# Means of lone rows as one TensorE product per group, and one VectorE division per four tiles, in layers 1 to 3 of a graph-attention kernel

## What is computed

```python
wh = x @ W
e = (wh @ a_src)[:, None] + (wh @ a_dst)[None, :]
e = leaky_relu(e)                                   # slopes 0.2, 0.01, 0.2, 0.01
attention = softmax(where(adj > 0, e, very_negative), axis=1)
out = attention @ wh                                # layer 1: + bias, no elu
x = layernorm(x + elu(out))                         # layers 0, 2, 3 with elu
```

## Time and profile before

| | us |
|---|---|
| median of 3 runs | 864.14 (862.48 to 875.75) |
| span of the profiled execution, first to last instruction | 608.0 |
| layer 0 with the making of the lists | 0 to about 288 of the span |
| layers 1, 2, 3 | about 288 to 404, 404 to 505, 505 to 608 |

### The profile page before, as it was taken

How to read it: one execution, slowest core, us unless ns; L and a number is a source line. 1 busy time by engine, 2 the same in 40 slices (tenths; PEclk the granted TensorE clock), 3 DMA queues, 4 the chain that set the end, 5 groups by cost and what they waited for, 6 DMA issues and landing times.

```text
span 608.0 us, 10701 instructions
## 1 busy us (share of the span) xinstructions
PE 394.4 (65%) x3404; PEld 321.7 (53%) x3404; DVE 366.7 (60%) x1696; ACT 398.5 (66%) x876; POOL 282.3 (46%) x296
## 2 busy tenths in 40 slices
PE   2165454443788548886627997755898876498773
PEld 1154333332576436865416886543787754397552
DVE  2104579965327898898321289854168984218996
ACT  3377876857437776696328588727588863858882
POOL 0000035746024234400777777377777467777710
PEclk9999999999999999999566999959899986899995
DMA  7998999969348861200221122122222113122210
GB/s 300 388 428 333 392 425 403 406 240 295 143 185 273 295 240 15 38 19 26 35 27 27 28 37 46 42 45 30 28 28 46 36 38 46 27 29 37 45 34 25
DMA packets 20547, 84.86 MB, mean 140 GB/s; under 512 B 6083, under 2 KB 11462, under 8 KB 16262
## 3 DMA queue, kind: packets, MB, share of 16 engines
q1 hardware_dynamic: 10102, 73.14, 30.7%
q0 software_dynamic: 9344, 9.89, 12.1%
q10 hardware_dynamic: 1040, 1.08, 0.5%
HBM read 78.72 MB, written 5.37 MB: 138 GB/s over the span
## 4 chain that ended last, share of the span: by engine, by line
DVE 29%; PE 20%; ACT 11%; issue 5%; POOL 3%; DMA 1%; ACTq 0%; DVEq 0%
PE bank L701 9%; DVE num L1252 4%; PE bank L686 4%; DVE arena L1221 3%; DVE x L1295 3%; POOL xg L525 3%; PE bank L669 3%; ACT arena L854 3%; ACT arena L840 3%; DVE stats L1277 3%; DVE lone L1238 2%; PE bank L667 2%; DVE mean_var L1280 2%; ACT arena L864 1%; ACT arena L828 1%
## 5 line engine op out<-in xcount | busy, mean ns | idle before, releaser
L525 POOL DMA_INDIRECT xg<-table,index x292 | 282.1, 966 | 298.2 <-DMA table<-wh 134.9
L828 ACT ACTIVATE arena<-arena,half 128x4096 bf16<-128x4096 int32 x31 | 114.5, 3701 | 18.8 <-DMA arena<-in_adj_t 18.3
L1221 DVE CUSTOM_DVE_ANT_0 arena<-bank,arena 128x256 f32<-128x256 f32 (+3 forms) x123 | 62.8, 521 | 101.3 <-ACT arena L840 101.2
L840 ACT ACTIVATE arena<-bank,sloped_own 128x256 f32<-128x256 f32 (+3 forms) x123 | 67.9, 556 | 53.1 <-PE bank L669 52.1
L701 PE MATMUL bank<-xg,arena 128*128 128x64 f32 x486 | 72.6, 284 | 24.3 <-ACT arena L864 22.6
L701 PEld LDWEIGHTS bank<-xg,arena 128*128 128x128 f32 x486 | 63.6, 197 | 35.3 <-ACT arena L864 31.2
L686 PE MATMUL bank<-packed,arena 128*128 128x128 f32 x339 | 64.7, 312 | 19.1 <-ACT arena L864 16.5
L1018 DVE MAX8 top<-bank 128x8 f32<-128x256 f32 x31 | 13.3, 430 | 84.4 <-PE bank L603 84.3
L669 PE MATMUL bank<-packed,xg 128*128 128x128 f32 x324 | 63.3, 298 | 0.0
L686 PEld LDWEIGHTS bank<-packed,arena 128*128 128x128 f32 x339 | 43.2, 158 | 30.8 <-ACT arena L854 25.6
L864 ACT COPY arena<-bank 128x256 f32<-128x256 f32 (+3 forms) x123 | 53.6, 443 | 6.8 <-PE bank L686 6.2
(11 more groups left out here) (141 smaller groups left out, 765.3 us busy)
## 6 DMA issues: line engine op xcount, KB each, us to landing
arena<-in_adj_t SPq DMA_DIRECT2D x31, 2048.0 KB, 11.0
xg<-table,index POOLq DMA_INDIRECT x292, 2.7
table<-wh SPq DMA_DIRECT2D x24, 132.0 KB, 1.7
arena<-in_adj SPq DMA_DIRECT2D x1, 2048.0 KB, 12.9
table<-wh ACTq DMA_DIRECT2D x1, 1056.0 KB, 25.7
x<-in_x SPq DMA_DIRECT2D x1, 1024.0 KB, 15.0
out_x<-x SPq DMA_DIRECT2D x8, 128.0 KB
packed<-in_c_packed SPq DMA_DIRECT2D x1, 306.0 KB
```

Of the source, the lines that this page charges most:

```text
L525: pool.indirect_dma_start(out=xg[:, c, :], out_offset=None, in_=table[l][0:rows, :], in_offset=bass.IndirectOffsetOnAxis(ap=index[:, c:c + ...
L828: nc.scalar.activation(masks[:, t % 2, :], arena[:, t % 3, :], ACT.Sign, bias=half[:, :]).then_inc(mask_made, 1)
L840: nc.scalar.activation(scores(l, n)[:, 0:m * P], score_ps[n % len(score_ps)][:, 0:m * P], ACT.Relu, bias=sloped_own[:, k:k + 1], scale=ALP ...
L1221: nc.vector.tensor_tensor_reduce(out=y, in0=score_ps[n % len(score_ps)][:, 0:m * P], in1=y, scale=-1.0, scalar=-FLOOR, op0=ALU.add, op1=AL ...
```

## The change

In layers 1 to 3 `lone` is no longer made and no longer added. Instead the first PE instruction of each group is one f32 product of a 32-row left side (which of the group's rows are lone, tile by tile) and a 32-row right side of 256 columns (the mean of wh, in the 64 columns of the own tile), which writes the whole sum bank of the group; the tiles' products are added to it. Since a lone row's denominator is 1 and its own sum 0, the division leaves the mean. DVE then divides all four tiles with one tensor_tensor of 128x256. The left sides of all eight groups are made once, in layer 0: PE turns `lonely`, and DVE spreads it over 32 x 1024 elements. `start_layer` makes the 32 x 256 right side instead of the mean row in layers 1 to 3, and no longer waits for itself. Layer 0 keeps `lone`. The packed constants grow by 12 columns (612 before). The core of the diff:

```diff
@@ aggregate
+                if l >= 1 and k == GROUP_START[l][k // GROUP] and c0 == 0:
+                    if ng % GROUPS == 0:
+                        pe.wait_ge(sum_copied, l + 1)
+                    nc.tensor.matmul(agg[:, 0:GROUP * F], lonely_rows[:, k // GROUP, :],
+                                     means[:, :, :].rearrange("p j f -> p (j f)"), start=True, stop=False)
                 pe.wait_ge(turned_copied, n + 1)
...
-                                         start=(c0 + c == 0), stop=(c0 + c == BLOCKS[k] - 1))
+                                         start=(c0 + c == 0 and l == 0),
+                                         stop=(c0 + c == BLOCKS[k] - 1 and (l == 0 or k % GROUP == GROUP - 1)))
@@ PE, layer 0, round OVER_ROUND
+                    pe.wait_ge(tile_0_lonely, 1)
                     pe.wait_ge(over_made, 1)
+                    nc.tensor.transpose(room_ps[0:TILES, P:2 * P], lonely[:, :], ident[:, :])
@@ combine
-                link(nc.vector.tensor_tensor(lone[:, h, :, :], sum_wh[...], lonely[...], ALU.mult))
+                if l == 0:
+                    link(nc.vector.tensor_tensor(lone[:, h, :, :], sum_wh[...], lonely[...], ALU.mult))
...
-                for j in range(GROUP):
-                    t = nc.vector.scalar_tensor_tensor(
-                        out=y[:, j, :], in0=agg_ps[...][...],
-                        scalar=den[:, j:j + 1], in1=lone[:, h, j, :], op0=ALU.mult, op1=ALU.add)
+                if l == 0:
...
+                else:
+                    t = nc.vector.tensor_tensor(
+                        y, agg_ps[GROUP_POS[l][g] % 2][:, 0:GROUP * F].rearrange("p (j f) -> p j f", j=GROUP),
+                        den[:, :].unsqueeze(2).broadcast_to([P, GROUP, F]), ALU.mult)
                 t.then_inc(agg_read, 1)
@@ start_layer
+                if l >= 1:
+                    nc.vector.scalar_tensor_tensor(
+                        out=means[:, :, :], in0=wh_ps[0:TILES, 0:F].unsqueeze(1).broadcast_to([TILES, GROUP, F]),
+                        scalar=1.0 / N, in1=of_tile[0:TILES, :].unsqueeze(2).broadcast_to([TILES, GROUP, F]),
+                        op0=ALU.mult, op1=ALU.mult).then_inc(sum_copied, 1)
+                    return
@@ DVE, layer 0, round OVER_ROUND + 1, behind the flag (L1357)
+                    nc.vector.tensor_tensor(
+                        lonely_rows, room_ps[0:TILES, P:2 * P].unsqueeze(1).broadcast_to([TILES, GROUPS, P]),
+                        of_group[0:TILES, :].unsqueeze(2).broadcast_to([TILES, GROUPS, P]), ALU.mult)
```

More of the change, by code:

```diff
@@ L239, in turned_before @@
     return max([m for m in range(max(0, n - 2), n) if turned_bank(m) == turned_bank(n)], default=-1) + 1
-CONST_WIDTHS = [P, P, P, CODE_W, NCH, MAXR, TILES, 3 * TILES]
+CONST_WIDTHS = [P, P, P, CODE_W, NCH, MAXR, TILES, 3 * TILES, GROUP, GROUPS]
 def pieces(b):
@@ L274, in gat_kernel @@
         packed = sb("packed", [P, sum(CONST_WIDTHS)], F32)
-        ident, ones, before_f, packer_f, slot_col, room_row, slot_base, limits_row = [
+        ident, ones, before_f, packer_f, slot_col, room_row, slot_base, limits_row, of_tile, of_group = [
             packed[:, sum(CONST_WIDTHS[:i]):sum(CONST_WIDTHS[:i + 1])] for i in range(len(CONST_WIDTHS))]
@@ L308, in gat_kernel @@
         cand = sb("cand", [P, 2, MAXB * BITS], F32)
+        lonely_rows = cand[0:TILES, 0, 0:GROUPS * P].rearrange("p (g r) -> p g r", g=GROUPS)
+        means = cand[0:TILES, 1, 0:GROUP * F].rearrange("p (j f) -> p j f", j=GROUP)
         nbr = sb("nbr", [P, MAXB], F32)
@@ L405, in gat_kernel @@
         sum_copied = sem("sum_copied")
+        tile_0_lonely = sem("tile_0_lonely")
         score_made = sem("score_made")
@@ L697, in aggregate @@
                     pe.wait_ge(agg_read, ng - 1 if ng >= GROUPS + 2 else ng)
+                at = agg_col(l, k)
+                if l >= 1 and k == GROUP_START[l][k // GROUP] and c0 == 0:
[3 more added lines that the diff above has]
+                                     means[:, :, :].rearrange("p j f -> p (j f)"), start=True, stop=False)
                 pe.wait_ge(turned_copied, n + 1)
-                at = agg_col(l, k)
                 for c in range(m):
@@ L1234, in combine @@
                     v.wait_ge(max_made, 1)
-                    link(nc.vector.tensor_scalar(lonely[:, DENSE:DENSE + 1], neg_max[:, DENSE:DENSE + 1], -FLOOR, None,
-                                                 ALU.is_ge))
+                    nc.vector.tensor_scalar(lonely[:, DENSE:DENSE + 1], neg_max[:, DENSE:DENSE + 1], -FLOOR, None,
+                                            ALU.is_ge).then_inc(tile_0_lonely, 1)
+                    v.wait_ge(tile_0_lonely, 1)
                 v.wait_ge(aggregated, group_end(l, g))
-                link(nc.vector.tensor_tensor(lone[:, h, :, :], sum_wh[:, :].unsqueeze(1).broadcast_to([P, GROUP, F]),
-                                             lonely[:, k0:k0 + GROUP].unsqueeze(2).broadcast_to([P, GROUP, F]), ALU.mult))
+                if l == 0:
+                    link(nc.vector.tensor_tensor(lone[:, h, :, :], sum_wh[:, :].unsqueeze(1).broadcast_to([P, GROUP, F]),
+                                                 lonely[:, k0:k0 + GROUP].unsqueeze(2).broadcast_to([P, GROUP, F]), ALU.mult))
                 several = max(SEGN[k0:k0 + GROUP]) > 1
@@ L1250, in combine @@
                 link(nc.vector.reciprocal(den[:, :], den[:, :]))
-                for j in range(GROUP):
-                    t = nc.vector.scalar_tensor_tensor(
-                        out=y[:, j, :], in0=agg_ps[GROUP_POS[l][g] % 2 if l >= 1 else 0][:, agg_col(l, k0 + j):agg_col(l, k0 + j) + F],
-                        scalar=den[:, j:j + 1], in1=lone[:, h, j, :], op0=ALU.mult, op1=ALU.add)
+                if l == 0:
+                    for j in range(GROUP):
+                        t = nc.vector.scalar_tensor_tensor(
+                            out=y[:, j, :], in0=agg_ps[0][:, agg_col(l, k0 + j):agg_col(l, k0 + j) + F],
+                            scalar=den[:, j:j + 1], in1=lone[:, h, j, :], op0=ALU.mult, op1=ALU.add)
+                else:
+                    t = nc.vector.tensor_tensor(
+                        y, agg_ps[GROUP_POS[l][g] % 2][:, 0:GROUP * F].rearrange("p (j f) -> p j f", j=GROUP),
+                        den[:, :].unsqueeze(2).broadcast_to([P, GROUP, F]), ALU.mult)
                 t.then_inc(agg_read, 1)
@@ L1468, in _constants @@
               rows(ROOM + [OFFSET[k] + UNITS[k] * UNIT for k in range(TILES)] +
-                   [HIGH_TO[k] * P if k < PARTED else N for k in range(TILES)])]
+                   [HIGH_TO[k] * P if k < PARTED else N for k in range(TILES)]),
+              p[:, None] % GROUP == np.arange(GROUP), p[:, None] // GROUP == np.arange(GROUPS)]
     return {
```

## The result

The changed kernel takes 856.56 us (median of 6 runs, 846.02 to 866.89); the kernel before, measured beside it, takes 862.96 us. The ratio is 0.9858, with a 95% interval from 0.9811 to 0.9905: 12.3 us less (0.0142 x 863), between 8 and 16. The forecast was 852.5 us, 11.6 us less, in a range from 846.5 to 861; the change counts as within 2%. So the forecast held. But the trace after the change showed at once that one of its premises was false, and the experiments found one step wrong (layer 1) and others mis-sized.

The account below looks back on a forecast made before the run. DVE is busiest, but ACT's elu part limits the gain in layer 2. Gains of 5.3 + 2.8 + 4.6 less 1.15 make 11.6 us off 864.1, giving 852.5 us; range 846.5 to 861.

Parts of the forecast that it names:

- The 256 us: Whole execution: 256.1 us were taken to lie around the 608.0 us span and were added unchanged to the forecast.
- the gathers' room: Tile 1's last gather lands 2.5 us before its spread; 1.6 us of that room is needed, so it holds.
- What DVE sheds: Each of 24 combines: L1238 goes (0.45 us), one 0.42 us division replaces 0.86; 0.89 us each, 21.4 at most.
- The product: PE, each group: 0.45 us, lower bound 0.11; paid in groups 0 and 1, hidden in gaps from group 2 on.
- Layer 1: ACT's idle 0.91 us fits the 0.89; the product delays by 0.15, groups 1 to 6 gain 0.74; 5.3 us in all.
- Layer 2: ACT's elu part cannot move; most groups gain 0.2 us, DVE then idling before L1274; 2.8 us in all.
- Layer 3: ACT makes no copies of x and wh, so six groups gain 0.57 us each; 4.6 us in all.
- Layer 0: No gain; an added DVE instruction of 1024 elements a row costs 1.15 us (0.1 to 1.23).
- DVE alone setting the period: Rival: everything DVE sheds in a combine comes off the time, gain 17.5 us, time 846.6; chance 0.14.
- The products paid in every group: Rival: PE's in-order rounds put products ahead of the spreads, gain 4.4 us, time 859.7; chance 0.13.
- The clock: Rival: the clock rises after the dense sums, costing 7.1 us a layer; about 867 us from two layers on; chance 0.07.
- The gathers: Rival: the two later layers start up to 2 us later because gathers come too late, time 856; chance 0.06.

Follow-up runs that it names:

- e3: Changed kernel with DVE's old work (the wide multiplication for lone, four divisions) put back in layers 1 to 3, PE keeping its products: ratio 1.002 to the kernel before.
- e0: The kernel before, with no edit, traced a second time: 862.48 us, of which 860.6 are the span.
- e2: Changed kernel with each product issued twice into the same bank, the second overwriting the first: 874.7 us, ratio 0.988 to the kernel before.
- e1: Changed kernel without its products, leaving out the means of lone rows in layers 1 to 3: 861.6 us, no ratio; layer 1 period 5.98 us.
- e5: Changed kernel with POOL's gathers in layers 2 and 3 replaced by plain SP loads of consecutive (wrong) rows: 703.5 us, ratio 0.808 to the kernel before.
- e11: Kernel before with a memset behind each gather in all four layers, a gather every 1.53 us in layers 1 to 3: 663.3 us, ratio 0.763.
- e6: Changed kernel with a POOL memset and wait behind each gather of layers 1 to 3, a gather every 1.44 us: 758.4 us, ratio 0.865.

## Why the prediction was right, and where it was not

**The 256 us.** "I put the same 256.1 us around the span" was wrong: they were pauses inside it. The sum survived because the pauses are in both kernels alike and e3 shows that the gain does not come from them; that they cancel so well is in part luck, since layers 1 to 3 take 533.3 us in e0's trace and 512.8 after the change, and layer 0 ends 20 us earlier in the first. What I should have seen is that 256 us around a span of 608 is itself a finding, not a constant. For the same reason the paragraph on the gathers' room (2.5 us, needed 1.6) argued about an execution that the timed ones were not like.

**What DVE sheds.** Right: 0.42 for the division, 0.45 for L1238; e3 gives the whole gain back with just these two. (That nothing so wide was shorter than 0.42 was misread: L1069 of the trace before, with 16-bit elements, takes 0.29.)

**The product.** 0.45 us was right for a product behind another one (0.43 in e2), and too small for the one that the kernel has, between products of other shapes: that holds PE for 0.62. The lower bound of 0.11, time going with rows, is out. The sentence of the Trainium skill ("TensorE: Matmul & The Clock Gate", Why this matters for your kernels), that a single product on 32 rows takes the time of one on 128, agrees with e2's 0.43 on 32 rows, beside the 0.45 scaled from 128, as far as one width can show.

**Layer 1** was the step that failed. I had the product delay PE by "about 0.15 (0.45 less what PE has in hand, an estimate)" and the period falling by 0.74; it fell by 0.49. Layer 1 has no elu part, so ACT leaves room; with 0.89 us less on DVE the period would be 5.98, as e1 shows. Both terms of the 0.15 were wrong: the product is 0.62 and not 0.45, and what PE has in hand is 0.21 and not 0.30, so 0.41 are paid. No row stands behind the 0.30; PE's slack has to be taken against the period that is forecast, 5.98, and not against the old one, 6.9. The path was another too: the delay reaches ACT in its slope, behind PE's spread, and not in the copy behind the projection. From the first to the last combine layer 1 fell from 49.1 us in the forecast's trace to 45.4 in e5, 3.7 us, where I had 5.3 for the layer.

**Layer 2.** 0.2 us a group was forecast, 0.16 came; DVE idles for ACT's elu part as said. No row shows the 0.06 that I took off for the signal; after the change L1292 starts 0.10 after L880 ends in every steady group, and with 0.10 the same sum gives 0.16. That the product is not the limit is shown (e1: 0.02). That ACT is, is read from 12.50 busy us of 13.50 and from DVE's wait, and was not tested by taking work from ACT. Last combine to last combine the layer fell by 101.4 - 98.4 = 3.0 us without pauses (forecast 2.8).

**Layer 3.** 0.57 forecast, 0.53 measured; the layer fell by 100.87 - 95.34 = 5.5 us, and what follows the last combine by 0.9 (8.2 to 7.3). Forecast 4.6 for both: I had given the first groups 0.3 us and they gained more.

**Layer 0.** The instruction of 1024 elements takes 1.20 us, and its group's period rises from 7.37 to 8.26, by 0.89; forecast 1.15.

**The sum** of what the pause-free stretches show, with e5 for the changed kernel, whose layers 2 and 3 load by SP: 3.7 + 3.0 + 5.5 + 0.9 - 0.9 = 12.2 us. That the measured 12.3 lies so near is luck (its interval is 8 to 16). So is a part of the forecast's 11.6: the errors of layers 1 and 3 cancelled.

**The rivals.** DVE alone setting the period falls with e1 and e3. The products paid in every group is right in layer 1 and wrong in layers 2 and 3. The clock did not turn against it: the dense sums of layer 2 took 7.36 us after the change, 7.26 before, both at a granted clock of 1.00. The gathers did not come too late: from layer 1 on PE does not wait for one after the change.

## What to carry to other kernels

When one engine is relieved, compare every other engine with the period that you forecast, not with the old one; the engine that receives the work is the first to look at. Price the work where it will stand in that engine's order: here 0.62 us and not 0.45. A difference of 30% between the timed runs and the span of the trace has to be explained before a change of 1% is argued from that trace. And a stretch where engines wait for "remote" or "issue" while POOL issues gathers back to back is worth an experiment with a little room between them: here it alone was worth some seventeen times the change (e11: 872.3 - 663.3 = 209.0 us against 12.3).

## What the runs showed of the hardware

While POOL issues indirect DMAs of 128 rows every 1.25 us (0.95 us each), PE gets through 68 instructions in 70 us, and ACT gets what PE has made some us late (8.7 in the rows shown); every 1.44 us it is 233; every 1.53 us 387, with hardly a delay left. As many plain DMAs from SP do no harm (369). But the rate is not enough by itself: one execution, the forecast's, had a gather every 1.25 us, no pauses, and 404 instructions in 70 us. The Trainium skill ("DMA: Bandwidth & Descriptors", SWDGE vs HWDGE vs iDMA) says that GpSimd itself writes the descriptors of its DMAs into rings in SBUF, and that DMAs issued from SP do not touch that path. That e5 has no pauses fits the second half; whether the rings have to do with them no run here shows, and the interference that the page names is with DVE and not with PE. Whether PE's products really end late, or only their signals arrive late, the records don't tell: the Trainium skill ("Perfetto Trace Analysis", Summary: the profiler window per engine type) says that the end of a TensorE instruction in a trace is an estimate and that the travel of a semaphore is not in it. The gaps in PE's own issue in e6 speak for the first. A product of 32 rows and 256 columns in f32 holds PE for 0.62 us between products of other shapes and adds 0.43 behind its like. Why the relief is so steep between 1.44 and 1.53 us, and why one recorded execution of the kernel before had no pauses at all, stays open.
